# A state-space layer and a mixture of experts on one core: biases folded into the weights of the expert products, and a new table of urgencies for the order of the work

## What is computed

```python
x = x + layernorm(ssm(layernorm(x)))            # x: 8 sequences x 512 steps x 128 channels
x = x + layernorm(moe(layernorm(x)))

def ssm(x):                                      # N = 16 states per channel
    xn = layernorm(x) * gamma + beta
    dt = softplus(xn @ W_dt.T + b_dt);  A = -exp(A_log)
    h[t] = exp(dt * A) * h[t-1] + dt * B_in[t] * xn[t]        # B_in = xn @ W_B.T
    y[t] = sum_n C_in[t, n] * h[t, :, n]                      # C_in = xn @ W_C.T
    return y + D_param * residual

def moe(x):                                      # 8 experts, the best two of each row
    gate = softmax(x @ gate_w + gate_b);  value, index = top_k(gate, 2)
    hidden = relu(x @ w1[e] + b1[e])             # 128 -> 512
    out[e] = hidden @ w2[e] + b2[e]              # 512 -> 128
    return value[0] * out[index[0]] + value[1] * out[index[1]]
```

## Time and profile before

| | |
|---|---|
| median of 3 runs | 464.36 us (462.55 to 464.83) |
| span of the profiled execution | 462.4 us; its own time is not given, the median is 2.0 us above it |
| PE busy | 414.8 us, of it 116.7 us of fillers (L1312) |
| DVE, ACT, POOL busy | 340.5, 329.2, 297.2 us |
| first and last second product of a tile | 182.2 us and 438.5 us |
| last scan ends | 306.2 us |
| last instruction's line | store of the eighth sequence, 462.4 us |

### The profile page before, as it was taken

One profiled execution on the slowest core, in us unless ns is written; L12 is line 12 of the kernel. 1 busy time (PEld: TensorE's weight loads), 2 busy tenths in 40 slices (PEclk: granted clock), 3 DMA queues, 4 the chain that ended last, 5 costly groups with the idle time before them and its releaser, 6 DMA issues.

```text
span 462.4 us, 9999 instructions
## 1 busy us (share of the span) xinstructions
PE 414.8 (90%) x2886; PEld 322.8 (70%) x2909; DVE 340.5 (74%) x823; ACT 329.2 (71%) x902; POOL 297.2 (64%) x220
## 2 busy tenths in 40 slices
PE   7099999998999999979999999999999999999930
PEld 2046556474455458877787798989998989899830
DVE  5989899999999999999999999943354015102165
ACT  3966586691488579778999978958768758766723
POOL 3069476482799977357998727997767770777720
PEclk9679999999999999999999999999999999999965
DMA  7799999996887869998899999738887986966341
GB/s 190 287 417 296 408 361 322 321 336 212 239 303 280 310 222 324 376 298 220 309 360 340 377 366 312 232 100 236 255 221 212 268 245 148 278 181 168 93 134 48
DMA packets 66596, 122.57 MB, mean 265 GB/s; under 512 B 7800, under 2 KB 38784, under 8 KB 62192
## 3 DMA queue, kind: packets, MB, share of 16 engines
q1 hardware_dynamic: 61504, 113.03, 74.3%
q0 software_dynamic: 4320, 8.89, 6.1%
q10 hardware_dynamic: 720, 0.01, 0.1%
HBM read 105.98 MB, written 15.92 MB: 264 GB/s over the span
## 4 chain that ended last, share of the span: by engine, by line
PE 37%; POOL 6%; ACT 4%; issue 4%; DVE 2%; DMA 1%; POOLq 0%; ACTq 0%; SPq 0%
PE out_ps L1348 14%; PE hid_ps L1336 7%; PE u_ps L1336 4%; PE y_ps L1252 3%; POOL ch L712 3%; PE y_ps L1312 2%; PE misc L1306 2%; ACT hid_t L912 2%; PE gx_ps L1336 2%; POOL yg_dram L755 1%; PE misc L1298 1%; DMA c_rep<-yg_dram 1%; POOL c_rep L744 1%; POOL slots_in L732 1%; ACT ab L851 1%
## 5 line engine op out<-in xcount | busy, mean ns | idle before, releaser
L712 POOL TENSOR_TENSOR ch<-hs,c_rep 128x1024 f32<-128x1024 f32 x64 | 151.1, 2365 | 74.2 <-DVE hs L1000 50.3
L1000 DVE TENSOR_TENSOR_SCAN hs<-ab,u_ps 128x512 f32<-128x512 f32 x128 | 150.2, 1205 | 0.1
L851 ACT ACTIVATE ab<-dt,decay 128x512 f32<-128x512 f32 x128 | 88.9, 720 | 41.5 <-DVE hs L1000 40.9
L1348 PE MATMUL out_ps<-w_f,hid_t 128*128 x736 | 101.0, 281 | 3.4 <-ACT ot L921 1.7
L1348 PEld LDWEIGHTS out_ps<-w_f,hid_t 128*128 128x128 f32 x736 | 90.5, 193 | 8.7 <-issue 6.6
L1312 PE MATMUL y_ps<-none 128*128 128x512 bf16 x379 | 92.2, 379 | 0.9
L732 POOL DMA_INDIRECT slots_in<-x,pos x64 | 63.8, 997 | 35.2 <-DVE expert L1104 19.8
L991 DVE TENSOR_TENSOR u_ps<-b_rep,gx_ps 128x512 f32<-128x512 f32 x128 | 81.5, 680 | 3.4 <-DMA b_rep<-rows_dram 3.4
L912 ACT ACTIVATE hid_t<-hid_ps,w_tile 128x128 f32<-128x128 f32 x224 | 63.7, 372 | 15.4 <-PE hid_ps L1336 14.9
L1252 PE MATMUL y_ps<-ident,ch 128*128 128x128 f32 x512 | 67.1, 274 | 2.4 <-POOL ch L712 2.0
L1252 PEld LDWEIGHTS y_ps<-ident,ch 128*128 128x128 f32 x512 | 57.7, 141 | 13.8 <-POOL ch L712 9.7
(11 more groups left out here) (142 smaller groups left out, 474.9 us busy)
## 6 DMA issues: line engine op xcount, KB each, us to landing
b_rep<-rows_dram SPq DMA_DIRECT2D x64, 512.0 KB, 6.3
c_rep<-rows_dram SPq DMA_DIRECT2D x32, 1024.0 KB, 8.3
w_tile<-w_rows SPq DMA_DIRECT2D x92, 258.0 KB, 3.9
xt<-slots_in SPq DMA_DIRECT2D x20, 258.0 KB, 4.6
slots_out<-ot SPq DMA_DIRECT2D x33, 128.0 KB, 4.2
slots_in<-w_f SPq DMA_DIRECT2D x2, 1483.5 KB, 13.5
x<-x SPq DMA_DIRECT2D x8, 256.0 KB, 5.4
out<-mix SPq DMA_DIRECT2D x8, 256.0 KB, 3.6
```

What stands on the lines that cost most here:

```text
L712: nc.gpsimd.tensor_tensor(ch[:, n % NCH], hs[:, n % NH], c_rep[:, r // 2, 2 * (r % 2):2 * (r % 2) + 2].rearrange("p n t -> p (n t)"), ALU. ...
L851: nc.scalar.activation(ab[:, i % NA], dt[:, b % 2], ACT.Exp, scale=decay[:, 2 * r + h:2 * r + h + 1]).then_inc(s["decayed"], 1)
L1000: nc.vector.tensor_tensor_scan(hs[:, n % NH, h * T:(h + 1) * T], ab[:, i % NA], u_ps[i % NU][:], 0.0, ALU.mult, ALU.add).then_inc(s["scann ...
L1348: last = nc.tensor.matmul(out_ps[:, j * D:(j + 1) * D], hid_t[:, q % NHT, c * P:(c + 1) * P], w2_f[:, bass.ds(e * HC * D + c * D, D)], sta ...
```

## The change

1. **b1.** The input of the experts has a layer norm without scale behind it, so its 128 channels sum to zero. The last channel is therefore left out and a one stands in its place; in the weights the last row is subtracted from each of the others, and the bias stands as the last row. Host code puts the bias rows in place; the subtraction is done on the chip, once for the 8 experts: SP loads all first weights (`w1_in`, two transfers of 1 MB), PE adds them and minus the last row in `misc` (`w1_mul`, two products of 512 columns per expert), ACT copies them back (`w1_copy`), and SP writes them to memory (`w1_out`, two of 1 MB), from where `tile_weights` loads. `w_tile` has no bias columns any more.
2. **One ReLU per tile**: 128 x 512 without bias in place of four of 128 x 128.
3. **Gate bias** likewise (`gate_less`, on POOL). DVE takes the maximum and subtracts it; one exponential of 128 x 32 on ACT replaces a small copy and four exponentials.
4. **b2** is cut on POOL into three bf16 parts (`b2_parts`; 5 small operations), which SP brings into one row each (`b2_in`). Each second product begins with one product of these 3 rows with ones (bf16, 128 columns). `weigh_turn`, `weigh_copy`, `bias_mix` and `chosen` are gone, and `mix_sum` begins with a plain multiplication.
5. Small buffers of the final norm are doubled; host code lays out the weights.
6. **The order**: new steps and durations in `COST`, and another number for every kind in `URGENCY`. `alone` comes out as 44 (34 before).

```diff
-                for c in range(HC):
-                    last = nc.scalar.activation(hid_t[:, q % NHT, c * P:(c + 1) * P], hidden(q)[:, c * P:(c + 1) * P],
-                                                ACT.Relu, bias=w_tile[:, q % NW, HID + c:HID + c + 1])
-                last.then_inc(s["hid_t_ready"], 1)
+                nc.scalar.activation(hid_t[:, q % NHT], hidden(q)[:], ACT.Relu).then_inc(s["hid_t_ready"], 1)
...
             def tile_down(q, _):
                 m = STORE_OF[q]
                 j = q - STORES[m][1]
-                pe.wait_ge(s["hid_t_ready"], q + 1)
                 if j == 0:
                     after(pe, s["tile_copied"], m)
                 e = picked.pop(q)
+                nc.tensor.matmul(out_ps[:, j * D:(j + 1) * D], ones_b[:], b2_s[:, bass.ds(e * D, D)], start=True, stop=False)
+                pe.wait_ge(s["hid_t_ready"], q + 1)
                 for c in range(HC):
...
-                                            w2_f[:, bass.ds(e * HC * D + c * D, D)], start=(c == 0), stop=(c == HC - 1))
+                                            w2_f[:, bass.ds(e * HC * D + c * D, D)], start=False, stop=(c == HC - 1))
...
+            def w1_mul(e, _):
...
+                misc_free("w1_mul", e + 1)
+                nc.tensor.matmul(misc[:], ident[:], w1_part(e // PART)[:, e % PART], start=True, stop=False)
+                nc.tensor.matmul(misc[0:D - 1, :], minus[:, e:e + 1].to_broadcast([E, D - 1]), last_row[:], start=False,
+                                 stop=True).then_inc(s["w1_ps"], 1)
...
+            def w1_in(i, _):
+
+                sp.dma_start(w1_part(i), w1_rows[PART * i:PART * (i + 1)].rearrange("e p h -> p e h")).then_inc(w1_loaded[i], 16)
+
+            def w1_out(i, _):
+
+                sp.wait_ge(s["w1_set"], PART * (i + 1))
+                sp.dma_start(w1_dram[PART * i:PART * (i + 1)].rearrange("e p h -> p e h"), w1_part(i)).then_inc(s["w1_out"], 16)
+
+            def b2_in(_, __):
+
+                sp.wait_ge(s["b2_parts"], 3)
+                for i in range(3):
+                    sp.dma_start(b2_s[i:i + 1, :].rearrange("p (e d) -> p e d", e=E), b2_part[:, i, :]).then_inc(s["b2_in"], 16)
...
+            pool.wait_ge(s["small"], 16 * 4)
+            nc.gpsimd.tensor_tensor(gate[0:D - 1], gate[0:D - 1], gate_last[0:D - 1], ALU.subtract).then_inc(s["gate_less"], 1)
+            nc.gpsimd.tensor_copy(b2_part[:, 0], b2_f[:]).then_inc(s["b2_parts"], 1)
+            pool.wait_ge(s["b2_parts"], 1)
+            nc.gpsimd.tensor_tensor(b2_rest[:, 0], b2_f[:], b2_part[:, 0], ALU.subtract).then_inc(s["b2_left"], 1)
...
                 for k in range(K):
-                    last = nc.vector.scalar_tensor_tensor(out=mix[:, b % NMIX, k], in0=yg(b)[:, k],
-                                                          scalar=weight[:, 0, K * b + k:K * b + k + 1],
-                                                          in1=misc[:, k * P:(k + 1) * P], op0=ALU.mult, op1=ALU.add)
+                    last = nc.vector.tensor_scalar(mix[:, b % NMIX, k], yg(b)[:, k], weight[:, 0, K * b + k:K * b + k + 1], None, ALU.mult)
...
-    "tile_send": 0, "tile_store": 12.5, "weigh_turn": 33, "weigh_copy": 22.5, "yg_load": 29.5, "gather": 22.5,
...
+    "tile_relu": 38.55, "tile_send": 17.45, "tile_store": 1.85, "tile_turn": 68.4, "tile_up": 19.65,
```

224 lines of the change are left out of this document (118 added, 106 removed).

## The result

The changed kernel takes 485.52 us (median of four runs, 481.96 to 489.91) against 463.46 us in the same session. The ratio is 1.044, with a 95% interval of 1.040 to 1.048: slower, where I had forecast 459.5 and a range up to 466.0. The four runs lie apart, two near 482.5 us and two near 489. The profiled execution has a span of 480.2 us at a granted clock of 0.975, where the kernel before has 0.959, so the clock isn't the reason.

A forecast was written before the change was run, and what follows sets the result against it. DVE bounds the kernel until the last scan, then PE until the last second product. Last scan at 315.7, last tile at 434.8 and an end of 22.8 gave a 457.6 us span (-4.8), so 459.5 us on the median; range 453.5 to 466.0.

The forecast's parts named there:

- the one on the b2 product: PE's tiles behind the last reduction: the added product takes 0.11 us in each of 49 tiles, +5.4 us.
- The head, 5.5 us: Before the first drive: two 1 MB loads and SP's wait for POOL delay it by 5.5 us, bounds 0 and 8.
- Last scan at 315.7: End of the scans: 306.2 plus 5.5 (head), 2.0 (write-back) and 2.0 (gathers) gives 315.7 us, between 306 and 324.
- From the last reduction on: Last reduction at 324.6 us to last tile: fewer products and bias work, 108.4 us, plus 1.8 for idle PE.
- Bias work, -7.8: PE behind the last reduction: five bias products (-5.6 us) and five turns of weights (-2.2) fall away.
- POOL's gathers: Among the scans: nine gathers in one piece, 11.7 us without weighing, delay the scans by 2.0 us, bounds 0 and 5.
- The last rival: Stage of the scans: POOL's piece of nine gathers stops the scans, 469 us; chance 0.13.
- ReLU, 0: PE's tiles: ReLU ends at 0.58 in place of 1.14 us, but PE waits little for ACT, so nothing counted.
- The second path: Last group's rows, routed and scattered: its first tile starts at 382.2 us, last ends at 432.1, level with the other path.
- The end, 22.8: Behind the last tile, sends, loads and mixing: 22.8 us, 1.1 less than before.
- The conditions for "wrong": Last scan before 310 or behind 321, last-group tiles 2.06 or 2.3 us, or PE waiting over 5 us for rows.
- The budget check: PE, first to last second product: fillers -8.0, bias work -7.8, b2 +10.1, sum -5.7 us against the paths' -3.7.

The follow-up runs named there:

- e6: Changed kernel with the bf16 b2 product over 128 rows, padded with zeros, in place of three rows; 467.22 us, ratio 1.004.
- f3: Changed kernel's order, b2 over 128 rows and loaded late, first weights not prepared, b1 and gate bias as in the kernel before; 471.12 us, ratio 1.016.
- e1: Changed kernel with the b2 product of every tile left out, so b2 is added nowhere; 458.81 us, ratio 0.989.
- e10: Changed kernel without the b2 product and without the preparation of the first weights; 454.63 us, ratio 0.978.
- e13: Kernel before, in its own order, without its bias work (routing-weight turns, copies and eight bias products); 460.54 us, ratio 0.992.
- e9: Changed kernel's computations in the order given by the urgencies of the kernel before, one gather among the scans instead of ten; 486.52 us, ratio 1.047.
- e4: Changed kernel with a tile's ReLU in four operations of 128 x 128 in place of one of 128 x 512; 482.85 us, ratio 1.041.
- f5: Changed kernel with the bf16 b2 product over 128 rows and four ReLUs of 128 x 128 a tile; 465.62 us, ratio 1.002.

## Why the prediction was wrong

The step that failed is the one on the b2 product: "I take 0.11, one of the eight passes of 0.89/8 that also have 128 columns and a weight load". Columns and weights were like those of the row, the number of rows was not, and no row that I had read showed so small a product between large ones in a steady run. The bounds (0.06 to 0.23) were those of whole products, so they left out what the neighbours lose. Measured: 0.11 over 128 rows (1.90 less 1.79 us), the very number, though by luck, since it is 0.06 at the product's place and 0.05 in the products behind it; and 0.35 over three (2.14 less 1.79); in the whole the three rows cost 18.3 us more than 128.

That is not all of the miss. e6 has the product at the price that I had put, and still takes 467.22 us, 0.4% more than the kernel before, not 1% less. Its span of 463.7 us is 6.1 above the forecast 457.6: the last scan ends 1.9 later (317.6), the last reduction another 2.2 later (328.7), the stretch from there to the last tile is 3.3 longer (113.5 for 110.2), and the end is 1.3 shorter. So of the 22.6 us between after's span and the forecast, 16.5 are the small product's and 6.1 other terms'; which of these fail, the points below say as far as the runs show it.

The Trainium skill, "TensorEngine Tiling (Array Packing)", section "Key Properties" under "Tiling Modes", says that a change of tiling mode drains TensorE, and its list of modes puts 64 rows and 32 rows apart from 128. I had not weighed it, since the code asks for no such mode. The trace agrees with it: 64 rows cost as much as three (485.0 and 485.5 us), and 128 rows 467.2; that such a change of mode is what happens inside is argued from this and not shown. Its page gives no price; by the rows here it is some 0.12 us for each change, half of 2.14 less 1.90. The figure of 56 ns that the prediction quoted from the Trainium skill, "TensorE: Matmul & The Clock Gate", section "What you observe", is also found, but between starts and with 128 rows only (0.06); with three it is 0.16.

Point by point:

- **The head, 5.5 us.** First drive at 23.14, as forecast. I took most of it for the transfer; the wait alone is as long. That the last scan loses what the first drive loses was wrong in the new order: f3's first drive came 5.4 us ahead of e6's and its scans ended no earlier.
- **Last scan at 315.7.** 325.5 in after, 317.6 with 128 rows, 315.2 without b2. The step that failed in it is the cover: I let what came ahead of the last reduction cost nothing but PE's fillers. The 17 products of tiles moved there are 15.1 us and the b2 products of 43 tiles 4.7 even at my price, while the 34 fillers taken away give 8.0 us and PE had 5.1 us idle. Between after and e6 it is 43 x 0.24 = 10.3 us by the tile, and 9.7 measured (last reduction 338.4 and 328.7). Reductions come late, and POOL waits for them (y_ps, 16.6 us; 4.1 in the kernel before, first fence below, after in the second), though e1, without the product, still has 12.0 us, and e10, without the preparation too, 5.4: only a part of it is the product's. DVE's scans themselves hardly wait (0.5 us in all). What holds DVE up before the last scan is, above all, the statistics of a summed sequence, which wait 7.7 us for PE's sums (0.2 in the kernel before); 3.3 us for the scattered rows and 3.1 for ACT come to it.

```profile
L712 POOL TENSOR_TENSOR ch<-hs,c_rep 128x1024 f32<-128x1024 f32 x64 | 151.1, 2365 | 74.2 <-DVE hs L1000 50.3 <-DMA c_rep<-rows_dram 19.1 <-PE y_ps L1252 4.1
```
```profile
L749 POOL TENSOR_TENSOR ch<-hs,c_rep 128x1024 f32<-128x1024 f32 x64 | 150.7, 2358 | 68.9 <-DVE hs L1043 36.7 <-PE y_ps L1289 16.6 <-DMA c_rep<-rows_dram 14.9
```

- **From the last reduction on.** Forecast 110.2 us to the last tile. Measured 120.4 in after, 113.5 in e6, 107.0 in e1. So of the product's surcharge 6.9 us lie here. The rest of the stretch falls short of the booking too: at my own price of the product, in e6, it is 3.3 us longer than forecast.
- **Bias work, -7.8.** Worth 3.3 (e13). Where it went, PE's waits for ACT's copies grew by 3.2 us, so a part of its time had covered another wait.
- **POOL's gathers.** No wait of DVE for POOL stands in the stage of the scans, so no stop, as forecast (the 2.0 us can't be told apart from the rest). The last rival fell with e9.
- **ReLU, 0.** Right in the new order (e4, f5), 2.4 us in the kernel before.
- **The second path.** The last group's rows were not what PE waited for: its longest idle time behind the last scan is 1.4 us, so the 1.8 us that I added for it were not needed in after.
- **The end, 22.8.** 21.4 us.
- **The conditions for "wrong".** Two came true: the last scan ended behind 321, and a tile took over 2.3 us. The 2.14 us are without turns and must not be held against my 2.17, which has them; by the measure of the earlier trace rows ten tiles of the last group take 441.90 - 418.23 = 23.67 us, 2.37 each.
- **The budget check** had all 92 tiles and came to -5.7 with +10.1 for b2. With the measured 92 x 0.35 = 32 it would have been +16.4, near the 19.6 us by which that stretch grew. So the budget, with the measured price, comes within about 3 us. It held the better view of PE than the sum by paths, and I read it as a confirmation.

Still open: why f3 is slower than e6 (3.9 us by the medians, 5.6 by the ratios), of which the clock near the end may be a part, how the 6 us between e13 and e10 divide, why the scans in e6 and f3 end at the same time with first drives 5.4 us apart, and what the preparation of the weights costs (the ratios say 5 to 6 us in both pairs, the profiled executions 1.8 and nothing). The sum of what was measured (e10's 454.6, 8.4 for b2, some us for b1) comes out at the time of the kernel before, so no version of this change is shown to be faster.

## What to carry to other kernels

Price an added small product by the number of its rows as well as by its columns, and look at the products on both sides of it: where it repeats once a tile, pad it with zeros to the rows of its neighbours, which costs memory and the filling (here on POOL in the head, where the first drive came 1.6 us later, 24.78 for 23.14). A cover of fillers must be counted against the whole of what goes into it (here 8 us of fillers for 15 us of moved tiles and another 15 us, 43 x 0.35, of the small product). When two delays overlap, undo both before saying that neither matters. And when the step that you suspect has been put right, hold what remains against the forecast again: here 6 us of the miss were left.
